# Inverse roots on ScalarE, 32x32 score and mask tiles, a last group in two, and a new order of a three-layer block

## The reference

```
x = x + layernorm(attention(layernorm(x)))        # 16 heads of 8, 4 key/value heads, causal, rotary
x = x + layernorm(two_layers(layernorm(x)))       # DEPTH = 2
layer: h = shift_token(x); q, k, v = split(h @ wqkv)           # 8 heads of 64
       q = l2norm(q) * q_scale; k = l2norm(k) * k_scale; rotary with a position scale
       x = x + softmax(8 q k^T, window of 64 back) v @ wo
       h = layernorm(shift_token(x)) * ln_g + ln_b; a, g = split(h @ w1 + b1)
       x = x + (a * gelu(g)) @ w2 + b2
```

## Time and profile before

| | |
|---|---|
| median of 3 runs | 502.34 us (502.02 to 503.59) |
| the profiled execution | 504.87 us, span 503.0 us |
| TensorE busy | 467.1 us, 5472 matmuls |
| VectorE, ScalarE, GpSimd busy | 376.5, 343.7, 317.0 us |
| mean granted TensorE clock | 0.978 of 2.4 GHz |

### The profile page before, as it was taken

The page is one execution under the profiler, slowest core; times in us unless marked ns, Lnnn a source line. Parts: engine busy times, 40 slices in busy tenths (PEclk is TensorE's granted clock), DMA queues, the critical chain, the costliest instruction groups (busy, mean ns, idle before and its releaser), DMA issues.

```text
span 503.0 us, 14088 instructions
## 1 busy us (share of the span) xinstructions
PE 467.1 (93%) x5472; PEld 292.8 (58%) x5472; DVE 376.5 (75%) x725; ACT 343.7 (68%) x906; POOL 317.0 (63%) x250
## 2 busy tenths in 40 slices
PE   8879999999999898999799989999999899999992
PEld 6555766675664566756545656655654466556641
DVE  3835684678775986899868796958888879868576
ACT  1135656565567788878886797788674888998632
POOL 2322251445979899779989865868669966564011
PEclk9979999999999989999999989999999999999996
DMA  5022022000001001010000010100010001011002
GB/s 149 2 91 89 7 45 46 4 3 3 4 2 44 3 1 22 3 43 3 1 22 2 22 23 1 24 1 22 3 22 21 20 5 23 2 23 22 2 8 76
DMA packets 13453, 11.43 MB, mean 23 GB/s; under 512 B 4194, under 2 KB 10700, under 8 KB 13388
## 3 DMA queue, kind: packets, MB, share of 16 engines
q1 hardware_dynamic: 13388, 10.54, 8.3%
HBM read 5.16 MB, written 1.05 MB: 12 GB/s over the span
## 4 chain that ended last, share of the span: by engine, by line
PE 71%; ACT 9%; DVE 8%; issue 6%; POOL 5%; DMA 1%; SPq 0%; ACTq 0%; DVEq 0%; POOLq 0%
PE bank L464 10%; PE bank L558 8%; PE bank L679 7%; PE bank L638 5%; ACT bank L1268 5%; PE bank L648 5%; PE bank L567 5%; PE bank L500 4%; PE bank L693 4%; PE bank L619 4%; PE bank L578 3%; PE bank L477 3%; PE bank L596 3%; PE bank L600 2%; POOL r_qk L2346 2%
## 5 line engine op out<-in xcount | busy, mean ns | idle before, releaser
L2346 POOL TENSOR_TENSOR r_qk<-ss,minus_half 128x16 f32<-128x16 f32 x32 | 93.7, 2929 | 2.7
L1268 ACT ACTIVATE bank<-bank,mn_b 128x128 f32<-128x128 f32 x256 | 88.8, 368 | 4.1 <-DVE mn_b L1818 4.0
L2339 POOL TENSOR_TENSOR rc<-rc,rs 128x1024 f32<-128x1024 f32 x32 | 75.5, 2360 | 21.3 <-DVE rs L1810 21.3
L1751 DVE TENSOR_REDUCE mx_a<-bank 128x2 f32<-128x512 f32 (+1 forms) x96 | 61.7, 685 | 32.2 <-PE bank L477 31.8
L1221 ACT ACTIVATE pT_k<-bank 128x512 f32<-128x512 f32 x96 | 52.9, 597 | 38.4 <-PE bank L477 38.4
L558 PE MATMUL bank<-wqkv,xS 128*128 128x512 f32 x128 | 62.6, 612 | 1.7 <-issue 1.1
L464 PE MATMUL bank<-qT_a 32*128 32x128 f32 (+1 forms) x1024 | 57.4, 351 | 6.6 <-DVE mx_a L1751 3.3
L2353 POOL TENSOR_TENSOR rc<-rc,r_qk 128x1024 f32<-128x1024 f32 x32 | 60.8, 1902 | 2.8
L1268 ACT ACTIVATION_READ_ACCUMULATOR bank<-bank,mn_b 128x1 f32 x256 | 60.2, 235 | 0.0
L464 PEld LDWEIGHTS bank<-qT_a 32*128 32x128 f32 x1024 | 41.0, 192 | 19.8 <-issue 9.5
L679 PE MATMUL bank<-yfT,w 128*128 128x512 f32 (+1 forms) x96 | 49.1, 612 | 0.3 <-ACT v_b L1251 0.3
(11 more groups left out here) (125 smaller groups left out, 849.7 us busy)
## 6 DMA issues: line engine op xcount, KB each, us to landing
v_b<-v_b SPq DMA_DIRECT2D x32, 128.0 KB, 2.3
wqkv<-in_L_ffn_wqkv_dram SPq DMA_DIRECT2D x2, 768.0 KB, 4.4
out_dram<-pT_k SPq DMA_DIRECT2D x4, 256.0 KB, 2.4
x_all<-in_L_attn_x_dram SPq DMA_DIRECT2D x1, 768.0 KB, 5.0
w<-in_L_ffn_w_dram SPq DMA_DIRECT2D x2, 341.0 KB
wo<-in_L_ffn_wo_dram SPq DMA_DIRECT2D x2, 256.0 KB, 4.6
const<-consts_dram SPq DMA_DIRECT2D x1, 352.0 KB, 4.5
x_all<-in_L_attn_x_dram SPq DMA_DIRECT2D x1, 256.0 KB, 2.8
```

Of the source, the lines that this page charges most:

```text
L1268: m = s.activation(x, x, ACT.Exp, bias=mn_b[:, qt, c, p:p + 1], scale=-1.0, accum_out=sum_b[:, qt, c, p:p + 1])
L1751: v.tensor_reduce(mx_a[:, qt, h0:h0 + nh], full(src).rearrange("p (h k) -> p h k", h=nh), AX.X, ALU.max).then_inc(S("a_mx"), 1)
L2339: g.tensor_tensor(rc[:, k % 2, :, :], rc[:, k % 2, :, :], rs[:, k % 2, :, :], ALU.add).then_inc(S("b_add"), 1)
L2346: g.tensor_tensor(r_qk[:, n, :], ss[:, n, :], minus_half[:, :], ALU.pow).then_inc(S("b_r"), 1)
```

## The change

- The power -0.5 of `b_pow`, `a_z` and `a_h0` leaves GpSimd. ScalarE computes exp(-0.5 ln v) in two small activations, the second of which waits for the first; the sum of squares is limited on VectorE, after the sum. `exps()` asks for a table that holds exponential and logarithm; it stands ahead of the first exponentials and after each run of gates. The power of the groups' norms and of the last norms stays on GpSimd.
- `a_turn` becomes `a_turn_k` (two 128x128 transposes) and `a_turn_q` (sixteen of 64 rows, to a pair of banks, one copy of 1024 columns on ScalarE). `a_turn_back` has sixteen of 64 rows, and `a_o` multiplies in two parts.
- The scores of a quad are made in 32x32 tiles, four times as many products with the same columns each. Masks are 32x32 tiles on the diagonal blocks. Blocks of 32 rows off the diagonal are masked within the score product by seven more rows: ones in the queries' columns, -1e30 in the keys' (the memsets of `a_pads`).
- `b_scores` uses 64x64 tiles for both units of a batch.
- Five buffers of turned queries and values, not three; two of the five lie in `p_b` and `pT_b`.
- The last group of two batches is cut: the second layer has groups of 2, 2, 2, 1 and 1 batches, and five stores.
- SP issues the first layer's attention weights ahead of the first maxima.
- The order of every engine's list, and the banks, are new.

The diff without the lists and without what only follows from these lines:

```diff
+A_BUFS = 5
...
-PAIRED = BATCHES // 2
+PAIRED = BATCHES // 2 + 1
...
+    q32, k32 = q % ROWS, np.arange(ROWS)[None, :]
+    c[:, C_MQ:C_MK] = packed(np.where(k32 > q32, NEG, 0))
+    c[:, C_MK:C_MB] = packed(np.where(q32 > k32, NEG, 0))
...
+        qT_a += [x[:, :, :, :, :].rearrange("p t c a k -> p (t c a k)")[:, 0:A_BLOCKS * SEQ]
+                 .rearrange("p (j q) -> p j q", q=SEQ) for x in (p_b, pT_b)]
...
+        def span(g):
+            if g < PAIRED - 2:
+                return 2 * g, 2, 0
+            return g + PAIRED - 2, 1, (g - PAIRED + 2) * TILES
...
+            load_attention(0)
+            maxima(0)
...
+            def a_turn_k(b, dst, *free):
+                if b == 0:
+                    t.wait_ge(S("a_pads"), 1)
...
+            def a_turn_q(b, pair, *free):
+                t.wait_ge(S("a_qk"), b + 1)
+                for f in free:
+                    after(t, *f)
+                w = PARTS // 2
+                for x in range(A_GROUP * TILES):
+                    j, n = x // TILES, x % TILES
+                    for h in range(2):
+                        r = slice(h * w, (h + 1) * w)
+                        m = t.transpose(full(2 * pair + h)[:, x * w:(x + 1) * w],
+                                        qk_a[r, n, j * A_KV:(j + 1) * A_KV, :].rearrange("p g r -> p (g r)"), ident[r, r])
+                m.then_inc(S("a_stq"), 1)
...
                 for i in range(nh):
-                    for n, (queries, v) in enumerate(pairs):
+                    for o in range(0, PARTS, ROWS):
+                        for n, (queries, v) in enumerate(pairs):
+                            for c in range(2):
+                                dst = full(banks[2 * n + c])[o:o + ROWS, i * w:(i + 1) * w]
+                                tile, h0, _ = use_q(v, c) if queries else use_k(v, c)
+                                g, j = h0 // A_GROUP, h0 % A_GROUP + i
+                                r = slice(g * ROWS, (g + 1) * ROWS)
+                                x = qT_a[k % A_BUFS] if queries else qT_a[(k - 1) % A_BUFS]
+                                own = slice(tile * PARTS + o, tile * PARTS + o + ROWS)
+                                if queries:
+                                    left, right = x[r, j, own], x[r, A_GROUP, 0:w]
+                                else:
+                                    left, right = x[r, A_GROUP, own], x[r, j, tile * PARTS:SEQ]
+                                t.matmul(dst, left, right, start=(i == 0), stop=False,
+                                         tile_position=(g * ROWS, o), skip_group_check=True)
+                for n, (queries, v) in enumerate(pairs):
+                    first = w - PARTS if queries else 0
+                    for j in range(PARTS // ROWS):
                         for c in range(2):
-                            dst = full(banks[2 * n + c])[:, i * w:(i + 1) * w]
-                            tile, h0, _ = use_q(v, c) if queries else use_k(v, c)
-                            g, j = h0 // A_GROUP, h0 % A_GROUP + i
-                            r = slice(g * ROWS, (g + 1) * ROWS)
-                            x = qT_a[k % 3] if queries else qT_a[(k - 1) % 3]
-                            own = slice(tile * PARTS, (tile + 1) * PARTS)
-                            if queries:
-                                left, right = x[r, j, own], x[r, A_GROUP, 0:w]
-                            else:
-                                left, right = x[r, A_GROUP, own], x[r, j, tile * PARTS:SEQ]
-                            t.matmul(dst, left, right, start=(i == 0), stop=False,
-                                     tile_position=(g * ROWS, 0), skip_group_check=True)
-                half = PARTS // 2
-                for n, (queries, v) in enumerate(pairs):
-                    for h in (1, 0) if queries else (0, 1):
-                        for c in range(2):
-                            r, o = slice((h ^ c) * half, (h ^ c) * half + half), slice(h * half, h * half + half)
+                            g = (use_q if queries else use_k)(v, c)[1] // A_GROUP
+                            r, o = slice(g * ROWS, (g + 1) * ROWS), slice(j * ROWS, (j + 1) * ROWS)
                             dst = full(banks[2 * n + c]).rearrange("p (h x) -> p h x", h=nh)
-                            if queries:
-                                dst, mask = dst[o, :, w - PARTS + h * half:w], mask_q[c][r, h * half:PARTS]
-                            else:
-                                dst, mask = dst[o, :, 0:(h + 1) * half], mask_k[c][r, 0:(h + 1) * half]
-                            m = t.matmul(dst, ident_h[r, r],
-                                         mask.unsqueeze(1).broadcast_to([half, nh, dst.shape[2]]), start=False, stop=True,
-                                         tile_position=((h ^ c) * half, h * half), skip_group_check=True)
+                            m = t.matmul(dst[o, :, first + j * ROWS:first + (j + 1) * ROWS], ident_h[r, r],
+                                         (mask_q if queries else mask_k)[r, :].unsqueeze(1).broadcast_to([ROWS, nh, ROWS]),
+                                         start=False, stop=True, tile_position=(g * ROWS, j * ROWS), skip_group_check=True)
                     m.then_inc(S("a_sc" if queries else "a_p2"), 1)
...
-            def a_turn_back(b, dst, *free):
+            def a_turn_back(b, pair, *free):
                 t.wait_ge(S("a_ov"), b * 2 + 2)
                 for f in free:
                     after(t, *f)
+                w = PARTS // 2
                 for n in range(TILES):
                     for g in range(A_KV):
-                        m = t.transpose(full(dst + n)[:, g * PARTS:(g + 1) * PARTS],
-                                        ovT[:, g, n * PARTS:(n + 1) * PARTS], ident)
+                        x = n * A_KV + g
+                        for h in range(2):
+                            r = slice(h * w, (h + 1) * w)
+                            m = t.transpose(full(2 * pair + h)[:, x * w:(x + 1) * w],
+                                            ovT[r, g, n * PARTS:(n + 1) * PARTS], ident[r, r])
...
-                    for w in range(qt + 1):
+                    for w in range(2):
                         for c in range(2):
                             r = slice(c * HD, (c + 1) * HD)
-                            dst = full(2 * pair + c)[:, p * PARTS:(p + 1) * PARTS]
-                            if qt == 0:
-                                t.matmul(dst, qk[r, 0, p, 0:PARTS], qk[r, 1, p, 0:PARTS],
-                                         start=(p == 0), stop=False, skip_group_check=True)
-                            else:
-                                q0, k0 = PARTS + w * WINDOW, (w + 1) * WINDOW
-                                t.matmul(dst[w * WINDOW:(w + 1) * WINDOW, :], qk[r, 0, p, q0:q0 + WINDOW],
-                                         qk[r, 1, p, k0:k0 + PARTS], start=(p == 0), stop=False,
-                                         tile_position=(c * HD, w * WINDOW), skip_group_check=True)
+                            dst = full(2 * pair + c)[w * WINDOW:(w + 1) * WINDOW, p * PARTS:(p + 1) * PARTS]
+                            q0, k0 = qt * PARTS + w * WINDOW, qt * (w + 1) * WINDOW
+                            t.matmul(dst, qk[r, 0, p, q0:q0 + WINDOW], qk[r, 1, p, k0:k0 + PARTS], start=(p == 0),
+                                     stop=False, tile_position=(c * HD, w * WINDOW), skip_group_check=True)
...
+            def exps():
+                s.preload_act_table_set("natural_log_exp_and_others")
+            def a_z_rs(b):
+                s.wait_ge(S("a_ve0"), b + 1)
+                s.activation(rs2[0][:, :], ve2[0][:, :], ACT.Ln).then_inc(S("a_ln0"), 1)
+                s.wait_ge(S("a_ln0"), b + 1)
+                s.activation(rs2[0][:, :], rs2[0][:, :], ACT.Exp, scale=-0.5).then_inc(S("a_rs0"), 1)
+            def a_h0_rs(b):
+                s.wait_ge(S("a_ve1"), b + 1)
+                s.activation(rs2[1][:, :], ve2[1][:, :], ACT.Ln).then_inc(S("a_ln1"), 1)
+                s.wait_ge(S("a_ln1"), b + 1)
+                s.activation(rs2[1][:, :], rs2[1][:, :], ACT.Exp, scale=-0.5).then_inc(S("a_rs1"), 1)
+            def b_pow(k):
+                n = k % 2
+                s.wait_ge(S("b_ss"), k + 1)
+                s.activation(ss[:, n, :], ss[:, n, :], ACT.Ln).then_inc(S("b_ln"), 1)
+                s.wait_ge(S("b_ln"), k + 1)
+                after(s, *unit("b_qkr", k - 2))
+                s.activation(r_qk[:, n, :], ss[:, n, :], ACT.Exp, scale=-0.5).then_inc(S("b_r"), 1)
...
+                if k < TILES:
+                    s.wait_ge(S("a_p2"), 5 * NQUAD)
...
-                    .then_inc(S("b_ss"), 1)
+                    .then_inc(S("b_sum"), 1)
+                v.wait_ge(S("b_sum"), k + 1)
+                v.tensor_scalar(ss[:, n, :], ss[:, n, :], TINY, None, ALU.max).then_inc(S("b_ss"), 1)
...
+            for i in range(SEQ // ROWS):
```

(74 more changed lines are left out.)

2557 lines of the change are left out of this document (1286 added, 1271 removed).

## The result

The changed kernel takes 541.75 us (median of 4 runs, 537.92 to 545.88) where the kernel before takes 502.43 in runs beside it: ratio 1.078, 95% interval 1.070 to 1.086. It is slower by 39 us; the forecast was 472. The profiled execution took 542.03 us, its span is 540.2.

A forecast was written before the change was run, and what follows sets the result against it. TensorE itself was taken to bound attention, GpSimd's chain the change of stage, latency the tail. Terms of -17 -3 -2 -2 -5 +2 -3 -1 +4 = -27, and -3 more, took 502.3 us to 472, range 456 to 489.

The forecast's parts named there:

- I take the burst: Score quads: load-and-multiply pairs issue at some 3.5 ns each, so 128 take 0.45 us, hidden behind 0.86 and 0.90 us rounds.
- Rival (1): Attention scores: dispatch binds the 32x32 quads; at 29 ns a pair 77 us more, about 549 us; chance 0.06.
- The wait between scores and masks: Score quads: masks in the scores' 32x32 shape remove the wait between them; shorter quads were counted at 17 us gained.
- Turns and window scores: Attention transposes and sliding-window scores: query and key turns gain 3 us, value turn back 2, window scores in 64x64 tiles 2.
- The inverse roots: Attention norms and rotary units: GpSimd loses 105 us of powers; ScalarE rises to about 371 us with 19 table loads.
- The gain of 5: Attention, 160:300: relieving GpSimd of the roots recovers 5 of the 12 us that TensorE idles there.
- The tail: After the last down-projection: the last group cut in two shortens 11.0 us to 8, 3 us less (1 to 4).
- the 4 us charged for new waits: Attention: with TensorE's part a fifth shorter, VectorE and ScalarE stand near 80%, so new waits add 4 us.
- the 3 for the order: Whole kernel: an order made for the new lengths and fewer scheduling gaps after shape changes gain 3 us more.
- the 1 for the clock: Start of attention, 16:40: less idling of TensorE may raise its granted clock and give back 1 us (0 to 3).
- score pairs 20 ns or more apart: Score quads: a sign named in advance that would show the forecast wrong.
- VectorE as releaser: Attention: a sign that the forecast is wrong, TensorE idle above 45 us with VectorE releasing it.

The follow-up runs named there:

- wide form: The changed kernel with score quads in four 32x128 tiles again, all else of the change kept; 491.03 us, ratio 0.9775 to the changed kernel.
- the bursts: The kernel before plus 1,536 one-column products in 32x32 tiles, 1,536 in 64x64 tiles and 1,024 waits, each ahead of a four-head quad's masks; 646.7 us, ratio 1.285.

## Why the prediction was wrong

**The step that failed** is the number of pairs a quad can issue: "I take the burst", 3.5 ns a pair, "so 128 pairs take 0.45 us and are hidden". The burst was real but 16 products, 32 pairs, long. The runs put two prices in its place. One is the pace inside a calm quad: after the first 33 pairs 8.3 ns a pair, with pauses of 0.19 and 0.11 us, in the four-head quad 13.5 ns a pair in all. The calm quads stand at 1.51 and 1.95 us against 1.25 and 1.31 wide, 0.26 x 32 + 0.64 x 16 = 18.6 us. I call it dispatch, since at 2.4 GHz one-column pairs of either tile shape keep the same 8 ns; what makes the pauses isn't shown. The other price is fetch: a block of 128 pairs each 3.45 to 4.0 us where they are wanted faster. A calm narrow quad with its masks has 80 pairs in 1.51 us, half again that rate, and "issue" on L513 and L524 is 25.1 us of waiting, 0.3 in the wide form. That this is fetch shows in the transfers: of these 25 waits 23, with 24.7 us, end 2.2 to 2.9 us after the transfer of a block began, as in the bursts. 18.6 + 24.8 = 43.4 of the 50.7 us. Nearly all the rest lies in the quads too: from their starts to the next other step they and their masks sum to 119.0 us, wide to 70.0, so 49.0 of the 50.7. Of the 5.6 us among them that neither price covers, the lower clock may be a part (in 40:80 it is 0.87 of 2.4 GHz, wide 1.00); that wasn't tried.

**The rival came near, in part by luck.** Rival (1) said 549 at 29 ns a pair, from the 32 pairs in 0.93 us of the earlier trace rows; measured 541.75. The direction and the mechanism, instructions that bind the quads, are right. The number is two errors that offset each other: 77 us for narrow tiles that cost 50.7, and 30 us of gains of which 11.5 came. And that row was bound by its stream, so that its 29 ns lie beside the 27 of a fetched burst is luck. I gave the rival 0.06, because that row "is explained by its stream". A row explained by one limit says nothing about the other, which may lie just beneath; 4,096p against 42 us asked for a measure of p over at least a block, and no row had one. Bounds of 3.5 and 29 ns that put the result on either side of zero deserved chances nearer to each other.

**The wait between scores and masks.** In the wide form, masks of another shape still start 1.08 to 1.10 us after the quad; in the narrow form some start among the scores. The wait did go with the shape, as said, but its gain drowned in the dispatch. What shortened quads was narrower masks: 0.11 x 32 + 0.25 x 16 = 7.5 us, where I had 17.

**Turns and window scores.** By the trace's records, summed over all steps from start to next start, wide form against before: turns of queries and keys 11.5 to 10.1 us (1.4 for 3), turn back 7.76 to 6.55 (1.2 for 2), window scores 44.8 to 42.4 (2.4 for 2). Right in kind, a little small.

**The inverse roots.** GpSimd 207.5 for "near 205", ScalarE 363.8 for 371, 19 table loads of 1,283 ns for 19, with 0.2 us of idle before nine together:

```profile
L1299 ACT ACT_TABLE_LOAD x9 | 11.5, 1283 | 0.2
L1380 ACT ACT_TABLE_LOAD x9 | 11.5, 1283 | 0.2
```

So the trace shows no drain ahead of the loads such as the 1380 ns that the Trainium skill ("ScalarE: Activation LUTs", "What ACT_TABLE_LOAD costs") adds to one. A logarithm and an exponential of 16 columns have rows now (wide form): 219 and 216 ns, for 0.22 taken. What they bring was mis-sized either way: in 200:300 TensorE is idle 7.2 us in the wide form and 7.7 before, VectorE 91.2 us busy; yet taking the roots back costs 18 to 20. The gain of 5 doesn't show as less idling; with GpSimd gone, VectorE is the fullest helper, as written.

**The tail.** From the end of the last down-projection to the end, 7.9 us for a forecast of 8 (11.0 before):

```profile
530.77 1.54 PE L745 MATMUL bank<-pT_k,w 128*128 128x256 f32 x6
```

**The sum of what is right** without the failed step: 7.5 + 1.4 + 1.2 + 2.4 + 3.1 = 15.6 us, of which 11.5 arrive in the wide form. TensorE's idle time there is 39.7 us for 35.9, so the 4 us charged for new waits came, and the 3 for the order, the 1 for the clock and the 3 net for the roots can't be seen. The account isn't closed: by the spans of the two profiled executions the wide form gains 15.2 us (503.0 to 487.8), with TensorE busy 19.0 less, of which the steps above are 12.5. Of what was to show each step, "score pairs 20 ns or more apart" is the sign that came (119.0 us of quads with their masks for 4,096 pairs, 29 ns each); VectorE as releaser was not.

## What to carry to other kernels

Splitting a product over smaller tiles multiplies TensorE's instructions: before the streams are counted, count load-and-multiply pairs (two to a float32 product) over every stretch of 4 us, and hold them under about 128 there; inside a step allow 8 to 14 ns for each pair behind the first 32. Both are estimates from the bursts and the calm quads here. A burst of a few starts bounds neither; only a row as long as the stretch in question does. Where a change has many parts, undo first the one that multiplies instructions: here it turned a gain of 2% into a loss of 8%. The version with 32x128 score tiles and all other parts of the change, 491.03 us, beats both kernels.

## What the runs showed of the hardware

- Instruction blocks of 16,384 bytes reach TensorE at best every 3.2 to 4 us (lowest spacing in the changed kernel 3.2; 29 blocks in 60:180 there, one in 4.1 us on average; 18 in the wide form). Time lost to them shows as "issue" among TensorE's own waits (25.1 us on scores and masks, wide 0.3), in no engine's busy share. The share of "issue" in the chain says less: the wide form has 10% without such pauses.
- TensorE runs on 2.2 to 2.9 us after the transfer of the block that it waits for began (23 pauses of the bursts, 23 of the changed kernel).
- One-column bf16 pairs start 8 ns apart inside a block; at 1.2 GHz this stays so in 32x32 tiles and becomes 13.3 in 64x64 ones. Float32 products of 32x32 tiles, two pairs each, start 6 to 8 ns apart for the first 16, then 16 to 17.
- 1,024 waits in a row on a count long reached cost TensorE 54.8 us: 512 instructions of 107 ns, 54 ns for each wait written.
- Products of other tiles overtake: masks start while scores queued ahead of them are still to start, as the timeline of the narrow quad shows.
